# Audio tower on one Trainium2 core: first input in smaller pieces, weights issued by ScalarE, batch norm's output made by GpSimd

## Chip, cores and metric

The kernel runs on one core of a Trainium2 chip. The metric is the device time of one execution in microseconds (us); lower is better. Times of several executions are given as their median.

## What is computed

The reference passes x, 16 sequences of 750 steps with 64 features, through five layers. Only the first is touched here; for a sequence it is

```python
win = jnp.concatenate([x[:, i:i + 746, :] for i in range(5)], axis=-1)
y = jax.nn.relu(jnp.einsum('btk,ok->bto', win, W) + b)
mean = jnp.mean(y, axis=(0, 1))
var = jnp.mean(jnp.square(y - mean), axis=(0, 1))
h = (y - mean) * jax.lax.rsqrt(var + EPS) * gamma + beta
```

The window is five steps, so 746 steps of 128 features come out of each sequence. Mean and variance are over all sequences and steps, so no output can be made before the last sequence has been convolved. Then follow four residual layers, each on a layer norm of h: a delta-rule attention, a mixture of experts in which experts choose tokens, a cross-attention to video, and a second mixture of experts with two experts per token.

## The kernel before, in words

Everything stays in one core's on-chip memory. The phases run one after another, and each phase is one or more blocks; in a block each engine has its own program, and all engines, SyncE included, meet at its end. The change is in `conv_phase`, which has two blocks; `norm_phase` (line 269), and with it the rest of the kernel, follows.

**First block: the convolution.** The features lie on the partitions. x is loaded twice, one step apart, on partitions 0 to 63 and 64 to 127 (lines 103 and 104), so that one matmul handles two of the five steps. `xw` is the place of x, laid over the tensor `h` that the second block fills. SyncE issues first the eight `first_loads` (line 99: two weight tiles of 128 partitions, a third in two halves of 64, then bias, gamma and beta with one number on each of 128 partitions, and the identity of 128x128, in this order), then x in four pieces of four sequences, two loads a piece, then some 40 `rest_loads` for later phases (line 106), and at last the `zeroed_loads` (line 109), which wait for two memsets of GpSimd. The small loads count up the semaphore `w_in`, each piece of x its own semaphore `x_in`, which reaches 32 when both loads have landed.

The matmuls run in a reduced-precision form, and weights and x are therefore split into a high and a low part; three products are summed. ScalarE makes the high part of each sequence (`high`, line 155), VectorE the low part by a subtraction (`low`, line 178), both in rings of three. At the start VectorE waits for all eight small loads, splits the weights (lines 184 and 187), and makes low parts only after that. TensorE waits for the split and for each low part. ScalarE applies bias and Relu out of the accumulation banks (line 167), VectorE takes statistics of each half sequence (line 196). At the end the statistics are aggregated (line 199), ScalarE takes the square root (line 170), and VectorE makes the scale and the shift in four short operations (lines 201 to 208).

**Second block: normalise and turn.** For each of the 16 sequences `yn = yT * scale + shift` is made (line 232, VectorE, two buffers), TensorE turns it by six transposes (line 249) into one of two halves of the banks, ScalarE copies it into `h` in two instructions (lines 262 and 264), and VectorE takes six statistics for the coming layer norm (line 226). VectorE's program puts the statistics of sequence b - 2 behind `yn` of sequence b. The semaphores: `tr_ps` tells that a sequence is turned, `yn_ready` that `yn` is there, `h_stored` that it is copied; `tr_ps` and `h_stored` begin at 2. GpSimd does one thing: it clears the unused rows of the last chunk of `h` (line 219), for which ScalarE waits (`pads`) before its first copy. SyncE waits there until all rest loads have landed.

Of the kernel before, what the change touches and what calls it, by code (L numbers as in the profile page):

```python
# [7 lines left out]
ALU = mybir.AluOpType  # L8
ACT = mybir.ActivationFunctionType
# [5 lines left out]
B = 16  # L15
T_IN = 750
CTX = 5
T = T_IN - CTX + 1
C = 128
NC = 6  # L20
# [17 lines left out]
EPS = 1e-5  # L38
# [33 lines left out]
def conv_phase(nc, k):  # L72

    stack, sb, sem = phase_scope(nc, k)
    with stack:
        yT = sb("yT", [P, B, T])
        yn = sb("yn", [P, 2, TP])
# [6 lines left out]
        bmv = sb("bmv", [P, 2])  # L84
        bsc = sb("bsc", [P, 4])
        xw = k.h[:].rearrange("p b c d -> p (b c d)")[:, 0:B * T_IN].rearrange("p (b t) -> p b t", t=T_IN)
        x_in = [sem(f"x_in{q}") for q in range(4)]
        w_in, rest_in = k.w_in, k.rest_in
        conv_ps, conv_relu, stats = sem("conv_ps"), sem("conv_relu"), sem("conv_stats")
        bn_chain, bn_sqrt = sem("bn_chain"), sem("bn_sqrt")  # L90
        yn_ready, tr_ps, h_stored, pads = sem("yn_ready"), sem("tr_ps"), sem("h_stored"), sem("pads")
        counted, zeroed = sem("c_counted"), sem("b2_zeroed")
        qb = B // 4

        with nc.Block() as block:
            @block.sync
            def _(sp):
                for ap, dram in k.first_loads:
                    sp.dma_start(ap, dram).then_inc(w_in, 16)
                for q in range(4):  # L100
                    s = slice(q * qb, (q + 1) * qb)

                    sp.dma_start(xw[0:64, s, :], k.xT[:, s, :]).then_inc(x_in[q], 16)
                    sp.dma_start(xw[64:128, s, 0:T_IN - 1], k.xT[:, s, 1:T_IN]).then_inc(x_in[q], 16)
                for ap, dram in k.rest_loads:
                    sp.dma_start(ap, dram).then_inc(rest_in, 16)
                sp.wait_ge(zeroed, 2)
                for ap, dram in k.zeroed_loads:
                    sp.dma_start(ap, dram).then_inc(rest_in, 16)
# [38 lines left out]
            @block.scalar  # L148
            def _(act):
                def high(b):  # L150
                    if b % qb == 0:
                        act.wait_ge(x_in[b // qb], 32)
                    if b >= RING:
                        act.wait_ge(conv_ps, 2 * (b - RING) + 2)
                    nc.scalar.activation(xh[:, b % RING, :], xw[:, b, :], ACT.Copy).then_inc(x_high, 1)

                act.wait_ge(edged, 1)
                for b in range(2):
                    high(b)
                act.wait_ge(w_in, 16 * len(k.first_loads))  # L160
                for b in range(B):
                    if b + 2 < B:
                        high(b + 2)
                    for half in range(2):
                        act.wait_ge(conv_ps, 2 * b + half + 1)
                        at, wide = EVEN[half]
                        nc.scalar.activation(yT[:, b, at:at + wide], k.ps[:, b % 2 * 2 + half, 0:wide], ACT.Relu,
                                             bias=k.conv_b[:, 0:1]).then_inc(conv_relu, 1)
                act.wait_ge(bn_chain, 1)
                nc.scalar.activation(bsc[:, 0:1], bmv[:, 1:2], ACT.Sqrt, bias=k.eps[:, 0:1]).then_inc(bn_sqrt, 1)  # L170

            @block.vector
            def _(dve):
                def low(b):
                    dve.wait_ge(x_high, b + 1)
                    if b >= RING:
                        dve.wait_ge(conv_ps, 2 * (b - RING) + 2)
                    nc.vector.tensor_tensor(xl[:, b % RING, :], xw[:, b, :], xh[:, b % RING, :].bitcast(F32),
                                            ALU.subtract).then_inc(x_low, 1)

                nc.vector.memset(k.eps[:], EPS)
                dve.wait_ge(w_in, 16 * len(k.first_loads))
                for j, w in enumerate((k.wc01, k.wc23, k.wc4)):
                    nc.vector.tensor_copy(wc[:, j, 0, :], w[:, :]).then_inc(w_split, 1)
                dve.wait_ge(w_split, 3)
                for j, w in enumerate((k.wc01, k.wc23, k.wc4)):
                    nc.vector.tensor_tensor(wc[:, j, 1, :], w[:, :], wc[:, j, 0, :].bitcast(F32),
                                            ALU.subtract).then_inc(w_split, 1)
                for b in range(2):
                    low(b)  # L190
                for b in range(B):
                    if b + 2 < B:
                        low(b + 2)
                    for half in range(2):
                        dve.wait_ge(conv_relu, 2 * b + half + 1)
                        nc.vector.bn_stats(bst[:, 2 * b + half, :],
                                           yT[:, b, half * HALF_T:(half + 1) * HALF_T]).then_inc(stats, 1)
                dve.wait_ge(stats, 2 * B)
                nc.vector.bn_aggr(bmv[:, :], bst[:].rearrange("p a s -> p (a s)")).then_inc(bn_chain, 1)
                dve.wait_ge(bn_sqrt, 1)  # L200
                nc.vector.reciprocal(bsc[:, 1:2], bsc[:, 0:1]).then_inc(bn_chain, 1)
                dve.wait_ge(bn_chain, 2)
                nc.vector.tensor_tensor(bsc[:, 2:3], bsc[:, 1:2], k.gamma[:, 0:1], ALU.mult).then_inc(bn_chain, 1)
                dve.wait_ge(bn_chain, 3)

                nc.vector.tensor_tensor(bsc[:, 0:1], bmv[:, 0:1], bsc[:, 2:3], ALU.mult).then_inc(bn_chain, 1)
                dve.wait_ge(bn_chain, 4)
                nc.vector.tensor_tensor(bsc[:, 3:4], k.beta[:, 0:1], bsc[:, 0:1], ALU.subtract).then_inc(bn_chain, 1)
                dve.wait_ge(bn_chain, 5)

        with nc.Block() as block:
            @block.sync
            def _(sp):
                sp.wait_ge(rest_in, 16 * (len(k.rest_loads) + len(k.zeroed_loads)))

            @block.gpsimd
            def _(pool):

                nc.gpsimd.memset(k.h[96:128, :, NC - 1, :], 0.0).then_inc(pads, 1)

            @block.vector
            def _(dve):
                def stats(b):
                    dve.wait_ge(h_stored, b + 3)
                    for c in range(NC):
                        last = nc.vector.bn_stats(k.st[:, b * NC + c, :], k.h[:, b, c, :])
                    last.then_inc(counted, 1)


                for b in range(B):  # L230
                    dve.wait_ge(tr_ps, b + 1)
                    nc.vector.tensor_scalar(yn[:, b % 2, 0:T], yT[:, b, :], bsc[:, 2:3], bsc[:, 3:4],
                                            ALU.mult, ALU.add).then_inc(yn_ready, 1)
                    if b >= 2:
                        stats(b - 2)
                for b in range(B - 2, B):
                    stats(b)
                dve.wait_ge(counted, B)

            @block.tensor  # L240
            def _(pe):
                pe.sem_inc(tr_ps, 2)
                with pe.Fori(0, PAIRS) as i:
                    for par in range(2):
                        pe.wait_ge(yn_ready, i * 2 + (par + 1))
                        pe.wait_ge(h_stored, i * 2 + (par + 1))
                        for c in range(NC):
                            n = rows(c)
                            last = nc.tensor.transpose(k.psf[0:n, par * 1024 + c * P:par * 1024 + (c + 1) * P],
                                                       yn[:, par, c * P:c * P + n], k.ident[:, :])  # L250
                        last.then_inc(tr_ps, 1)

            @block.scalar
            def _(act):
                act.sem_inc(h_stored, 2)
                act.wait_ge(pads, 1)
                with act.Fori(0, PAIRS) as i:
                    for par in range(2):
                        b = i * 2 + par
                        act.wait_ge(tr_ps, i * 2 + (par + 3))  # L260
                        o = par * 1024
                        nc.scalar.activation(k.h[:, b, 0:NC - 1, :],
                                             k.psf[:, o:o + 5 * P].rearrange("p (c d) -> p c d", d=P), ACT.Copy)
                        nc.scalar.activation(k.h[0:LAST, b, NC - 1, :],
                                             k.psf[0:LAST, o + 5 * P:o + 6 * P], ACT.Copy).then_inc(h_stored, 1)
# [2140 lines left out]
```

## Time and profile before

| | us |
|---|---|
| median of 3 executions | 2277.52 |
| lowest, highest | 2276.15, 2278.78 |
| the profiled execution: its own time | 2272.64 |
| its span | 2270.8 |

```profile
span 2270.8 us, 54560 instructions
...
PE 2000.0 (88%) x20890; PEld 1776.8 (78%) x20890; DVE 1607.0 (71%) x4095; ACT 1070.6 (47%) x2698; POOL 604.2 (27%) x650
```

PE is TensorE's matmuls, PEld its weight loads, DVE VectorE, ACT ScalarE, POOL GpSimd, SP SyncE; a "q" behind a name is the engine's sequencer. All times in the trace are counted from the start of the span. Neighbouring instructions of one kind are merged in a timeline; "x6" behind them is their number, and the duration is that of all of them together. What stands in brackets is how long the engine sat idle before, and who released it. These shares are over the whole span; the two blocks in question take the first 105 us of it, so the busy shares of the whole say little about them.

### The profile page before, as it was taken

The page shows a single profiled execution, that of the slowest core. Times are in us where ns is not written, and L with a number is a line of the kernel's source. Part 1 is how long each engine was busy: PE and PEld are TensorE (multiplying, and loading weights), DVE is VectorE, ACT ScalarE, POOL GpSimd, SP SyncE. Part 2 cuts the span into 40 slices and gives each one's busy share as a digit, 9 for nine tenths or more (in the row PEclk, how much of TensorE's full clock was granted, in tenths as well). Part 3 has the DMA queues.
Part 4 walks back from the last instruction along what each step waited for, and adds up shares of the span by engine and source line. Part 5 has one row for each costly group of instructions (what it writes and reads, how often), then busy time and mean ns, then how long its engine had stood idle before and what let it go on. Part 6 is the DMA issues. An engine that isn't in the chain of part 4 may idle for free. (4 is left out here: it accounts for less than half of the span.)

```text
span 2270.8 us, 54560 instructions
## 1 busy us (share of the span) xinstructions
PE 2000.0 (88%) x20890; PEld 1776.8 (78%) x20890; DVE 1607.0 (71%) x4095; ACT 1070.6 (47%) x2698; POOL 604.2 (27%) x650
## 2 busy tenths in 40 slices
PE   6589999989646988886999999976999999999998
PEld 5488777778534877885777777766999999999998
DVE  4755555654583855565999999986777777777774
ACT  4433333332344555552677766743444444444443
POOL 0002222220015555520343333343212222221220
PEclk9899999999877999997999999997999999999999
DMA  8100000000211111100000000000000000000000
GB/s 185 44 1 12 11 12 11 12 10 1 73 56 38 44 34 39 41 18 1 3 3 3 3 3 3 3 2 1 8 14 7 7 7 14 7 7 14 7 8 15
DMA packets 80355, 44.50 MB, mean 20 GB/s; under 512 B 45801, under 2 KB 74025, under 8 KB 79753
## 3 DMA queue, kind: packets, MB, share of 16 engines
q1 hardware_dynamic: 74248, 29.53, 5.7%
q0 software_dynamic: 5888, 12.07, 2.0%
q8 instruction: 136, 2.23, 0.4%
q14 instruction: 83, 0.67, 0.1%
HBM read 27.20 MB, written 14.38 MB: 18 GB/s over the span
## 5 line engine op out<-in xcount | busy, mean ns | idle before, releaser
L2127 ACT ACTIVATE w<-banks,b 128x384 f32<-128x384 f32 (+1 forms) x512 | 259.6, 572 | 392.9 <-PE banks L2201 392.9
L2183 PE MATMUL banks<-w,w 128*128 128x128 f32 (+1 forms) x3072 | 364.1, 275 | 0.0
L2183 PEld LDWEIGHTS banks<-w,w 128*128 128x128 f32 (+1 forms) x3072 | 350.4, 189 | 9.1 <-issue 8.7
L1710 PE MATMUL banks<-qT,w 64*64 64x128 f32 (+1 forms) x4608 | 267.9, 269 | 13.2 <-DVE eb L1612 8.7
L1710 PEld LDWEIGHTS banks<-qT,w 64*64 64x64 f32 x4608 | 247.3, 134 | 31.0 <-issue 20.8
L1718 PE MATMUL banks<-eb,w 64*64 64x128 f32 (+1 forms) x4608 | 268.9, 270 | 1.0 <-DVE eb L1612 1.0
L1681 POOL TENSOR_TENSOR t<-eb 128x768 f32<-128x768 f32 x96 | 171.8, 1789 | 289.0 <-ACT eb L1658 286.4
L1718 PEld LDWEIGHTS banks<-eb,w 64*64 64x64 f32 x4608 | 244.1, 133 | 1.7 <-DVE eb L1612 1.5
L2024 DVE SCALAR_TENSOR_TENSOR h<-banks,t_wt,h 128x128 f32 (+3 forms) x672 | 183.6, 342 | 83.2 <-PE banks L2183 79.7
L1237 POOL DMA_INDIRECT xg<-xs,rowu x184 | 178.4, 970 | 131.7 <-DMA xg<-xs,rowu 87.8
L1612 DVE TENSOR_TENSOR eb<-eb,rd 128x1536 f32<-128x1536 f32 x96 | 210.9, 2196 | 2.3 <-ACT rd L1669 2.3
L2199 PE MATMUL banks<-t_xh,t_w1h 128*128 128x384 f32 (+1 forms) x512 | 182.5, 356 | 0.2 <-ACT w L2106 0.2
L2201 PE MATMUL banks<-t_xh,t_w1l 128*128 128x384 f32 (+1 forms) x512 | 171.5, 335 | 0.0
L2200 PE MATMUL banks<-t_xlo,t_w1h 128*128 128x384 f32 (+1 forms) x512 | 171.0, 334 | 0.0
L1607 DVE TENSOR_REDUCE nm<-banks 128x128 bf16<-128x1536 f32 x96 | 162.8, 1696 | 11.3 <-PE banks L1710 11.3
L2067 POOL TENSOR_TENSOR t_rstd<-t_nv,t_minus_half 128x6 f32<-128x6 f32 x48 | 63.7, 1326 | 399.6 <-DVE t_nv L1925 398.2
L1658 ACT ACTIVATE eb<-banks 128x512 f32<-128x512 f32 (+1 forms) x288 | 147.1, 586 | 0.5
L1183 DVE SCALAR_TENSOR_TENSOR x_yl<-banks,gates,x_yh 128x128 fp32r<-128x128 f32 x184 | 51.9, 344 | 134.1 <-ACT x_yh L1330 134.1
L1428 PE MATMUL banks<-x_sel,x_yh 128*128 128x374 f32 (+1 forms) x384 | 120.1, 395 | 2.1 <-DVE x_sel L1191 1.1
L1191 DVE TENSOR_SCALAR x_sel<-iota,place 128x748 fp32r<-128x748 f32 x184 | 105.2, 625 | 5.1 <-PE banks L1428 5.0
L729 ACT ACTIVATE DT<-banks 128x768 f32<-128x768 f32 x60 | 48.7, 811 | 123.4 <-PE banks L822 123.4
L1428 PE MATMUL banks<-x_sel,x_yl 128*128 128x374 f32 (+1 forms) x384 | 99.3, 340 | 0.0
(305 smaller groups left out, 4241.9 us busy)
## 6 DMA issues: line engine op xcount, KB each, us to landing
out<-h SPq DMA_DIRECT2D x16, 320.0 KB
xs<-r_xl SPq DMA_DIRECT2D x16, 192.0 KB, 2.6
h<-in_xT SPq DMA_DIRECT2D x4, 750.0 KB, 15.7
h<-in_xT SPq DMA_DIRECT2D x4, 749.0 KB, 18.6
xg<-xs,rowu POOLq DMA_INDIRECT x184, 2.5
xs<-r_xl SPq DMA_DIRECT2D x16, 128.0 KB
blocks<-NT SPq DMA_DIRECT2D x24, 48.0 KB, 1.9
D<-blocks SPq DMA_DIRECT2D x24, 48.0 KB, 2.0
```

The source lines that it names most:

```text
L1237: nc.gpsimd.indirect_dma_start(out=xg[:, 4 * g + j, :], out_offset=None, in_=k.xs, in_offset=bass.IndirectOffsetOnAxis(ap=rowu[:, col:col ...
L1428: last = nc.tensor.matmul(k.ps[:, 5 + s, 0:TW // 2], y[lo:hi, col % 8, :], sel[lo:hi, col % SEL, s * (TW // 2):(s + 1) * (TW // 2)], start ...
L1612: nc.vector.tensor_tensor(eb[:, w % 4, :, 0:m], eb[:, w % 4, :, 0:m], rd[:, w % 2, None, 0:m].to_broadcast([P, FR, m]), ALU.mult).then_inc ...
L1681: nc.gpsimd.tensor_tensor(t1[:, n % 2, 0:m, :].rearrange("p t v -> p v t"), e[:, 0:6, 0:m], e[:, 6:12, 0:m], ALU.add).then_inc(tree, 1)
L1710: last = nc.tensor.matmul(lbanks(n)[place(n, hd), v, 0:wide(n)], k.Kt[half(hd), v, :], qT[half(hd), n // NC % 2, (n % NC) * P:(n % NC) * P ...
L1718: last = nc.tensor.matmul(k.ps[half(hd), 6, 0:wide(a)], k.Vd[place(a, hd), v, half(hd)], eb[place(a, hd), a % 4, v, 0:wide(a)], start=(v = ...
L2024: last = nc.vector.scalar_tensor_tensor(out=hh, in0=k.psf[0:n, o:o + P], scalar=wt[0:n, par, c * E1 + e:c * E1 + e + 1], in1=hh if e else ...
L2127: nc.scalar.activation(gb[u % 2][:, f, s * GW:s * GW + NFREE[s]], k.ps[:, order.bank(n), 0:NFREE[s]], ACT.Relu, bias=k.b1_1[:, 2 * e + f:2 ...
L2183: last = nc.tensor.matmul(k.psf[0:n, o:o + P], gb[u % 2][:, f, c * P:c * P + n], k.w2_1[:, 2 * e + f, :], start=(f == 0), stop=(f == 1))
L2199: nc.tensor.matmul(ps, w1h[:, 2 * e + f, :], xh[:, g, 0:w], start=True, stop=False)
L2200: nc.tensor.matmul(ps, w1h[:, 2 * e + f, :], xlo[:, g, 0:w], start=False, stop=False)
L2201: nc.tensor.matmul(ps, w1l[:, 2 * e + f, :], xh[:, g, 0:w], start=False, stop=True).then_inc(full, 1)
```

## The change

In the first block SyncE issues x at once, in pieces of 1, 1, 2, 4, 4 and 4 sequences (12 loads). ScalarE issues the eight small loads as the first thing in its program, then waits for `eps` and takes a square root of it into a place that is overwritten later, and goes on as before. In the second block GpSimd makes `yn` for all 16 sequences. VectorE clears the unused rows of `h` and then only takes statistics.

```diff
--- before.py
+++ after.py
@@ -84,21 +84,20 @@
         bmv = sb("bmv", [P, 2])
         bsc = sb("bsc", [P, 4])
         xw = k.h[:].rearrange("p b c d -> p (b c d)")[:, 0:B * T_IN].rearrange("p (b t) -> p b t", t=T_IN)
-        x_in = [sem(f"x_in{q}") for q in range(4)]
+        x_in = [sem(f"x_in{q}") for q in range(6)]
         w_in, rest_in = k.w_in, k.rest_in
         conv_ps, conv_relu, stats = sem("conv_ps"), sem("conv_relu"), sem("conv_stats")
         bn_chain, bn_sqrt = sem("bn_chain"), sem("bn_sqrt")
         yn_ready, tr_ps, h_stored, pads = sem("yn_ready"), sem("tr_ps"), sem("h_stored"), sem("pads")
         counted, zeroed = sem("c_counted"), sem("b2_zeroed")
-        qb = B // 4
+        CUTS = (0, 1, 2, 4, 8, 12, B)
+        eps_set = sem("c_eps")
 
         with nc.Block() as block:
             @block.sync
             def _(sp):
-                for ap, dram in k.first_loads:
-                    sp.dma_start(ap, dram).then_inc(w_in, 16)
-                for q in range(4):
-                    s = slice(q * qb, (q + 1) * qb)
+                for q in range(len(CUTS) - 1):
+                    s = slice(CUTS[q], CUTS[q + 1])
 
                     sp.dma_start(xw[0:64, s, :], k.xT[:, s, :]).then_inc(x_in[q], 16)
                     sp.dma_start(xw[64:128, s, 0:T_IN - 1], k.xT[:, s, 1:T_IN]).then_inc(x_in[q], 16)
@@ -148,12 +147,16 @@
             @block.scalar
             def _(act):
                 def high(b):
-                    if b % qb == 0:
-                        act.wait_ge(x_in[b // qb], 32)
+                    if b in CUTS:
+                        act.wait_ge(x_in[CUTS.index(b)], 32)
                     if b >= RING:
                         act.wait_ge(conv_ps, 2 * (b - RING) + 2)
                     nc.scalar.activation(xh[:, b % RING, :], xw[:, b, :], ACT.Copy).then_inc(x_high, 1)
 
+                for ap, dram in k.first_loads:
+                    act.dma_start(ap, dram).then_inc(w_in, 16)
+                act.wait_ge(eps_set, 1)
+                nc.scalar.activation(bsc[:, 0:1], k.eps[:, 0:1], ACT.Sqrt)
                 act.wait_ge(edged, 1)
                 for b in range(2):
                     high(b)
@@ -178,7 +181,7 @@
                     nc.vector.tensor_tensor(xl[:, b % RING, :], xw[:, b, :], xh[:, b % RING, :].bitcast(F32),
                                             ALU.subtract).then_inc(x_low, 1)
 
-                nc.vector.memset(k.eps[:], EPS)
+                nc.vector.memset(k.eps[:], EPS).then_inc(eps_set, 1)
                 dve.wait_ge(w_in, 16 * len(k.first_loads))
                 for j, w in enumerate((k.wc01, k.wc23, k.wc4)):
                     nc.vector.tensor_copy(wc[:, j, 0, :], w[:, :]).then_inc(w_split, 1)
@@ -216,7 +219,10 @@
             @block.gpsimd
             def _(pool):
 
-                nc.gpsimd.memset(k.h[96:128, :, NC - 1, :], 0.0).then_inc(pads, 1)
+                for b in range(B):
+                    pool.wait_ge(tr_ps, b + 1)
+                    nc.gpsimd.tensor_scalar(yn[:, b % 2, 0:T], yT[:, b, :], bsc[:, 2:3], bsc[:, 3:4],
+                                            ALU.mult, ALU.add).then_inc(yn_ready, 1)
 
             @block.vector
             def _(dve):
@@ -227,13 +233,8 @@
                     last.then_inc(counted, 1)
 
 
+                nc.vector.memset(k.h[96:128, :, NC - 1, :], 0.0).then_inc(pads, 1)
                 for b in range(B):
-                    dve.wait_ge(tr_ps, b + 1)
-                    nc.vector.tensor_scalar(yn[:, b % 2, 0:T], yT[:, b, :], bsc[:, 2:3], bsc[:, 3:4],
-                                            ALU.mult, ALU.add).then_inc(yn_ready, 1)
-                    if b >= 2:
-                        stats(b - 2)
-                for b in range(B - 2, B):
                     stats(b)
                 dve.wait_ge(counted, B)
```

## Rows read from the trace of the kernel before

**Rows 1.** Busy time by stretches of 10 us; columns as in the first line

```profile
core 0: us, PE busy (x) PEld busy (x) DVE busy (x) ACT busy (x) POOL busy (x), PEclk, DMA share, GB/s
...
10.00:20.00 10.00, 1.27 (x4) 1.30 (x5) 2.36 (x3) 3.55 (x4) 0.00 (x0) 1.00 1.03 214
20.00:30.00 10.00, 10.00 (x50) 8.44 (x50) 4.02 (x7) 3.52 (x6) 0.00 (x0) 1.00 1.08 225
...
80.00:90.00 10.00, 5.25 (x36) 3.76 (x36) 10.00 (x42) 5.35 (x13) 0.00 (x0) 1.00 0.00 0
```

**Rows 2.** Timeline, 0 to 32 us: start, duration, engine, line, work; SPq issues loads

```profile
0.72 2.15 SPq L99 DMA_DIRECT2D wc<-in_L_tok_WT  x4
...
4.50 0.43 SPq L99 DMA_DIRECT2D ident<-in_ident  x1
4.97 0.47 SPq L103 DMA_DIRECT2D h<-in_xT  x1
...
6.51 1.35 DVE L184 CAST c_w<-wc 128x128 fp32r<-128x128 f32 x3 [5.66 <-DMA ident<-in_ident]
...
7.90 0.70 DVE L187 TENSOR_TENSOR c_w<-wc,c_w 128x128 fp32r<-128x128 f32 x3
...
15.48 1.28 ACT L155 ACT_TABLE_LOAD   x1 [15.48 <-DMA h<-in_xT]
...
16.78 2.27 ACT L155 ACTIVATE c_xh<-h 128x750 fp32r<-128x750 f32 x3
17.64 2.64 DVE L178 TENSOR_TENSOR c_xl<-h,c_xh 128x750 fp32r<-128x750 f32 x3 [9.05 <-ACT c_xh L155]
...
18.73 0.65 PE L132 MATMUL banks<-c_xh,c_w 128*128 128x374 f32 x1 [18.73 <-DVE c_xl L178]
```

**Rows 3.** Timeline, end of the convolution; last line: SyncE's waits, us in total, times, longest

```profile
65.64 0.36 SPq L109 DMA_DIRECT2D gate<-in_L_ffn_gate_weight  x1
...
69.78 1.28 ACT L170 ACT_TABLE_LOAD   x1
70.38 1.02 DVE L199 BATCH_NORM_AGGREGATE bmv<-bst 128x2 f32<-128x192 f32 x1
71.44 0.29 ACT L170 ACTIVATE bsc<-bmv,eps 128x1 f32<-128x1 f32 x1 [0.37 <-DVE bmv L199]
...
SPq L95 <- PEq L95: 6.8, 1, 6.8
```

**Rows 4.** Timeline, the second block

```profile
73.01 1.80 POOL L219 MEMSET h<- 32x2048 f32 x1 [65.30 <-POOLq L95]
...
78.17 1.26 DVE L226 BATCH_NORM_STATS2 st<-h 128x6 f32<-128x128 f32 x6 [0.64 <-ACT h L264]
...
79.91 1.25 DVE L226 BATCH_NORM_STATS2 st<-h 128x6 f32<-128x128 f32 x6
79.93 0.70 ACT L262 ACTIVATE h<-banks 128x640 f32 x1 [0.82 <-PE banks L249]
...
81.07 0.70 ACT L262 ACTIVATE h<-banks 128x640 f32 x1 [0.26 <-PE banks L249]
...
100.74 3.57 DVE L226 BATCH_NORM_STATS2 st<-h 128x6 f32<-128x128 f32 x18
```

**Rows 5.** Line 232 by itself: duration ns min/median/max, first and last start us

```profile
L232 DVE TENSOR_SCALAR yn<-yT,bsc x16: 648/652/2034, 73.2 to 100.2; 128x746 f32<-128x746 f32 x16
```

**Rows 6.** DMA from 8 to 16 us

```profile
DMA packets 368, 1.73 MB, mean 216 GB/s; under 512 B 32, under 2 KB 32, under 8 KB 288
```

**Rows 7.** The small loads of line 99, all eight

```profile
DMA to landing us min/median/max: 1.8/2.0/2.2
```

**Rows 8.** GpSimd's instructions by line and shape: count, busy us, mean ns, idle before

```profile
L1681 POOL TENSOR_TENSOR t<-eb 128x768 f32<-128x768 f32 x80 | 146.8, 1835 | 251.6 <-ACT eb L1658 249.0 <-DVE den L1603 2.6
L2067 POOL TENSOR_TENSOR t_rstd<-t_nv,t_minus_half 128x6 f32<-128x6 f32 x48 | 63.7, 1326 | 399.6 <-DVE t_nv L1925 398.2
...
L1469 POOL COPY vD<-vT 128x768 f32<-128x768 f32 x1 | 0.8, 823 | 58.9 <-ACTq L1464 58.9
```

## The prediction

> **What bounds the kernel now.** The change touches only the first two blocks of one phase, so the first view is the busy time by stretches of 10 us [rows 1]. Three things are to be seen. From 10 to 20 us TensorE does 1.27 us of work while the DMA engines are full: the start waits for data. From 20 to 30 us TensorE is busy all the time: the convolution is TensorE's. From 80 to 90 us VectorE is busy 10.00 of 10.00 us and TensorE about half: the second block is VectorE's. GpSimd is empty in all three.
>
> Second, the timeline of the start [rows 2]. SyncE issues eight small loads (weights, bias, gamma, beta, identity) from 0.72 to 4.93 us, and only then, from 4.97 us, eight loads of x, two for each piece of four sequences. The weights are there at 6.51 us, when VectorE starts to split them, and the split ends at 8.60 us. ScalarE waits for the first piece until 15.48 us, then loads an activation table for 1.28 us, and makes the first high part at 16.78 us; VectorE's first low part starts at 17.64 us and TensorE at 18.73 us. So x is last, with weights ready 9 us before.
>
> Third, the end of the convolution [rows 3]. ScalarE's table load for the square root (69.78 to 71.06 us) lies beside the last statistics and their aggregation, which ends at 71.40 us; the square root starts at 71.44 us. That load costs nothing today. SyncE had issued its last load at 66.0 us and waited 6.8 us for the others at the block's end: the first thing that could take over from a faster convolution.
>
> Fourth, the second block [rows 4, 5]. Each sequence costs VectorE a TENSOR_SCALAR and six statistics, and the pattern repeats every 1.74 us (78.17 to 79.91 us), 16 times; the last statistics end at 104.31 us.
>
> **Part 1: the start.** The x loads leave SyncE at 0.72 instead of 4.97 us, 12 issues now, and the first piece is one sequence (0.375 MB) instead of four (1.5 MB). The x stream ran at 1.73 MB in 8 us, 216 GB/s [rows 6], so 0.375 MB need 1.7 us alone, 3.5 us at half the rate. Small loads landed 2.0 us after issue [rows 7]; from 2.7 us on, the first sequence is in at 4.4 to 6.2 us. ScalarE has first to issue eight loads (4.2 us by SyncE's own row), load the table (1.28 us) and take one square root (0.29 us), which ends at about 6.5 us; its first high part (0.83 us) can end by about 7.5 us. The table load has moved from the path to a place where it is hidden behind the weights. If Copy or Relu needed another table, the 1.28 us would go into the same cover, or, before the first Relu, into the time that TensorE takes for the first sequence.
>
> So the **weights** become last: VectorE needs 2.1 us of splitting after them and 1.1 us from the first low part to TensorE [rows 2]. When they land the trace cannot say, because it has no such stretch. Lower end: 6.5 us as before, start at 9.7 us, 9.0 us won. Upper end: the eight loads have 896 partition rows (six of 128, two of 64), a packet each, 56 on each of 16 engines, and each waits for one packet of x; x packets took 8 us x 16 / 368 = 0.35 us [rows 6], so 56 x 0.35 = 19.5 us, landing near 22 us, start near 25.2 us, 6.5 us lost. I take a value near the lower end: by bytes the weights are 0.26 MB, at half the rate 2.4 us, less than the 4.2 us that their issue takes, so only the last one's wait counts: 8 packets per engine, each behind 3000 bytes of x (3000 bytes x 16 / 216 GB/s = 0.22 us), 1.8 us. With 2.0 us of latency the identity, issued at 4.5 us, lands at 8.3 us; I round to 8.5 us. TensorE then starts at 8.5 + 2.1 + 1.1 = 11.7 us: **7.0 us won**.
>
> [...]
>
> What follows doesn't shorten: the 16 sequences take 3.2 us each (18.7 to 70.4 us [rows 2, 3]), while x arrives every 1.75 us, so later pieces of 4 are early. The chain from last statistics to scale and shift keeps its length. SyncE's issues: x now streams from 2.7 instead of about 7 us but shares with the weights, so I expect its end to move by about 2.5 us, to 63.5 us; the block would end at 66.0 + 6.8 - 7.0 = 65.8 us. The cover is 2.3 us, and nearly gone if the weights land at 6.5 us: about 9 us is the most this part can give.
>
> **Part 2: the second block.** VectorE loses 16 TENSOR_SCALARs (0.65 us each [rows 5]) and takes one memset that GpSimd did in 1.80 us [rows 4]; ScalarE needs it only with its first copy 4 us into the block, so it is hidden. VectorE's 96 statistics remain: 18 in 3.57 us, 1.19 us per sequence. ScalarE's copies come every 1.14 us where they hardly wait (79.93 to 81.07 us). GpSimd now makes yn, with no row of its own for this operation. Lower end: its copy of 128x768, 0.82 us [rows 8]. Upper end: its two-input operation, 1.84 us for 768 elements [rows 8], so 1.79 us for 746. I take 1.0 us, nearest to the copy, because it too reads one tensor; with 0.1 us for the wait GpSimd's 1.1 us stays below VectorE's 1.2 us, so the exact value doesn't matter up to there. Its wait for transposes two sequences back holds nothing else, for its queue is otherwise empty.
>
> First sequence: today yn was ready at 75.2 us (its 2.03 us, beside GpSimd's memset, where the others take 0.65 [rows 5]), and the first statistics began 2.95 us later. Now GpSimd runs beside VectorE's memset; I allow it until 75.0 us. Statistics from 77.9 us, 16 x 1.2 = 19.2 us, end 97.1 us on the old clock, against 104.3: **7.2 us won**. With a first yn at 74.1 us it would be 8.1 us.
>
> **Sum:** 7.0 + 7.2 = 14.2 us. The profiled execution took 2272.64 us (2270.8 us of span and 1.8 us around it), 4.9 us below the median; the same difference taken from the median 2277.52 gives **2263.3 us**. Everything after waits at the blocks' ends, so I carry the sum through whole. The runs spread by 2.6 us; I count 0.2% (4.6 us) as what can be told from no change.
>
> **Rivals.**
> A, weights late: the packet-by-packet turn above. For it: 56 packets on each engine against a stream that fills them; against it: nothing but the small bytes. -6.5 + 7.2 = 0.7 us won, 2276.8 us. Chance 0.10.
>
> B, GpSimd becomes the bound: 1.79 us each. 73.2 + 16 x 1.89 = 103.4 us for the last yn, + 3.5 us for its transposes, copies and statistics (today from 100.8 to 104.3 us) = 106.9 us, 2.6 us later than today. 7.0 - 2.6 = 4.4 us won, 2273.1 us. For it: the only arithmetic on GpSimd near this size is the two-input row; against it: this operation reads half as much. At 1.4 us each 10.6 us would be won. Chance 0.17. [...]
>
> C, slower: GpSimd works through multiply and add as two passes, 2 x 1.79 = 3.58 us. 73.2 + 16 x 3.68 + 3.5 = 135.6 us, 31.3 us later; with 7.0 us won at the start 24.3 us slower, 2301.8 us. The time turns slower by 0.2% from 2.35 us each (73.2 + 16 x 2.45 + 3.5 = 115.9 = 104.3 + 7.0 + 4.6). For it: a power of only 6 elements takes GpSimd 1.33 us [rows 8], so an operation's kind can cost more than its size; against it: multiply and add are the simple kinds of its other rows. Chance 0.05.
>
> The change doing less than it says (another table load at the end or the start) is hidden, as shown.
>
> **Numbers.** Forecast 0.66; the remaining 0.02 is mishaps. Faster: the forecast, two thirds of B, and the part of A in which the weights land between the ends, 0.80; same 0.14; slower 0.06. Range: 9.0 + 8.1 us won and 2 us of spread give 2258; B and its spread give 2274; A's end and C stay outside.
>
> **To be seen afterwards.** TensorE's first matmul near 11.7 us and VectorE's first cast near 8.5 us right; a first cast past 15 us is A. The last statistics of the second block 24 us after its start; VectorE's statistics waiting for ScalarE's copy, and these for transposes waiting for GpSimd, is B or C, with GpSimd's mean as the price. If SyncE's last issue comes after the convolution's last statistics, the start's gain was capped there. An untouched part that changes its length by over 2 us would make the forecast wrong in a way I have not counted.

## The result: 5 us won where 14 were forecast

| | before | changed |
|---|---|---|
| median of 13 executions each | 2275.94 us | 2269.53 us |
| lowest, highest | 2269.11, 2278.97 | 2265.55, 2275.72 |
| the profiled execution, its span | 2270.8 | 2267.7 |
| first operation of the layer norm behind the two blocks | 105.23 us | 97.26 us |

The ratio on record is 0.9977, with a 95% interval of 0.9967 to 0.9988: 5.2 us (2.7 to 7.5) less, faster by just more than what I had set as telling (4.6 us). A ratio on record is not the quotient of the two medians, here 0.9972, and can differ from it by up to 0.001; gains of whole kernels are read from the ratios throughout. The time lies inside the forecast's range, but the change won less than half of the 14.2 us forecast, and by another balance. The two halves went opposite ways: the start lost, the second block won more than forecast.

The start of the changed kernel, from its timeline:

```profile
0.74 0.61 SPq L102 DMA_DIRECT2D h<-in_xT  x1
0.74 2.16 ACTq L157 DMA_DIRECT2D wc<-in_L_tok_WT  x4
...
4.67 0.67 ACTq L157 DMA_DIRECT2D ident<-in_ident  x1
...
5.37 1.28 ACT L159 ACT_TABLE_LOAD   x1 [5.37 <-issue]
...
6.77 0.81 ACT L154 ACTIVATE c_xh<-h 128x750 fp32r<-128x750 f32 x1
...
8.02 0.83 ACT L154 ACTIVATE c_xh<-h 128x750 fp32r<-128x750 f32 x1 [0.43 <-DMA h<-in_xT]
...
17.17 0.83 ACT L154 ACTIVATE c_xh<-h 128x750 fp32r<-128x750 f32 x1 [8.33 <-DMA ident<-in_ident]
17.17 1.35 DVE L187 CAST c_w<-wc 128x128 fp32r<-128x128 f32 x3 [16.30 <-DMA ident<-in_ident]
...
19.17 2.63 DVE L181 TENSOR_TENSOR c_xl<-h,c_xh 128x750 fp32r<-128x750 f32 x3
...
20.25 0.65 PE L131 MATMUL banks<-c_xh,c_w 128*128 128x374 f32 x1 [20.25 <-DVE c_xl L181]
```

The answer to [rows 2]. x is there early: ScalarE has its table by 6.65 us and the high parts of the first two sequences by 8.85 us. Then it sits for 8.33 us, and VectorE for 16.30 us, and the row names the load of the identity for both. VectorE splits from 17.17 us, against 6.51 us before, and TensorE starts at 20.25 us, 1.5 us *later* than before. The DMA view of the first 18 us shows why. A queue's row has its packets, its MB and the share of the 16 DMA engines' time that the packets took; the last number of a load is its time in us from issue to landing (of two loads the median):

```profile
q1 hardware_dynamic: 913, 3.32, 83.9%
q10 hardware_dynamic: 1024, 0.26, 8.5%
...
wc<-in_L_tok_WT ACTq DMA_DIRECT2D x2, 64.0 KB, 2.6
...
wc<-in_L_tok_WT ACTq DMA_DIRECT2D x2, 32.0 KB, 4.4
ident<-in_ident ACTq DMA_DIRECT2D x1, 64.0 KB, 12.5
...
conv_b<-in_L_tok_b ACTq DMA_DIRECT2D x1, 0.5 KB, 5.7
gamma<-in_L_tok_gamma ACTq DMA_DIRECT2D x1, 0.5 KB, 6.9
beta<-in_L_tok_beta ACTq DMA_DIRECT2D x1, 0.5 KB, 9.6
```

A second queue, q10, carries the small loads: 1024 packets, 0.26 MB. Its tiles land 2.6 and then 4.4 us after issue, bias 5.7, gamma 6.9, beta 9.6, the identity 12.5 us, where all eight took 1.8 to 2.2 us before [rows 7]. The same view from 10 to 14 us:

```profile
q1 hardware_dynamic: 117, 0.75, 87.4%
q10 hardware_dynamic: 122, 0.05, 7.7%
```

Queue against queue, 117 and 122 packets: one for one, though x's packets carry 0.75 MB and the small ones 0.05 MB. Elsewhere it was not one for one: from 2 to 6 us the view has 434 small packets to 307 of x, from 6 to 10 us 339 to 240, and from 14 to 17.2 us, with the last small ones, 52 to 217. From 2 to 17.2 us that is 947 to 881. The counts are over all 16 engines; no view shows one engine alone.

The end of the convolution and the second block, to be held against [rows 3 to 5]:

```profile
61.99 0.36 SPq L108 DMA_DIRECT2D gate<-in_L_ffn_gate_weight  x1
...
71.25 1.02 DVE L202 BATCH_NORM_AGGREGATE bmv<-bst 128x2 f32<-128x192 f32 x1
...
73.22 0.16 DVE L211 TENSOR_TENSOR bsc<-beta,bsc 128x1 f32<-128x1 f32 x1
74.13 1.94 POOL L224 TENSOR_SCALAR yn<-yT,bsc 128x746 f32<-128x746 f32 x2 [55.75 <-SPq L214]
74.37 1.76 DVE L236 MEMSET h<- 32x2048 f32 x1 [0.99 <-PEq L96]
...
77.75 18.99 DVE L232 BATCH_NORM_STATS2 st<-h 128x6 f32<-128x128 f32 x96 [1.61 <-ACT h L265]
...
97.26 0.33 DVE L298 TENSOR_TENSOR n0tmp<-st 128x96 f32<-128x96 f32 x1 [0.52 <-PEq L214]
```
```profile
L224 POOL TENSOR_SCALAR yn<-yT,bsc x16: 969/970/979, 74.1 to 90.5; 128x746 f32<-128x746 f32 x16
```

GpSimd makes all 16 yn in 0.97 us each. VectorE's 96 statistics, once they start, follow without a gap, 18.99 us, from 77.75 to 96.74 us. The block lasts 22.6 us from GpSimd's first operation, where it took 31.3. The layer norm starts 8.0 us earlier: 8.7 from the block and 0.4 from its end (the norm's first operation waits 0.52 instead of 0.92 us), less 0.9 us for the later convolution and 0.2 us at the passage between the blocks. The length of the second block repeats within 0.3 us in every run; the 0.9 us does not. With the start untouched, the run of the second block alone (below) had its scale and shift ready at 70.41 us, 2.1 us before the kernel before (72.51 us): such is the scatter of one execution's first block.

### The profile page after: what moved, and what is told of

Read it like the earlier page. It is cut to its first block and busy times, and to the rows that moved or that the text cites. A ratio compares the mean times of both kernels' runs of the same rounds, so it can differ in the third digit from the quotient of the medians.

```text
span 2267.7 us, 54558 instructions
## 1 busy us (share of the span) xinstructions
PE 2002.6 (88%) x20890; PEld 1778.6 (78%) x20890; DVE 1598.9 (71%) x4080; ACT 1068.2 (47%) x2698; POOL 617.8 (27%) x665
## 3 DMA queue, kind: packets, MB, share of 16 engines
q0 software_dynamic: 5888, 12.07, 2.0%
q10 hardware_dynamic: 1024, 0.26, 0.1%
```

## The experiments

Theory 1: the small loads wait because each DMA engine serves the two queues in turn, a packet of one for a packet of the other. Theory 2: x's load of the memory, whatever the packets, or being issued by ScalarE, holds them. Theory 3: part of the gain is lost in later phases. Ratios and single times are to be held against runs of the kernel before on the same chip, whose median was 2269.84 us beside the first four kernels, 2275.16 us (one run) beside the single pieces and the half packets, and 2270.13 us beside the last five.

### One half at a time

The second block alone: the kernel before with the second block of the changed one.

```diff
second block of the kernel before:
-                nc.gpsimd.memset(k.h[96:128, :, NC - 1, :], 0.0).then_inc(pads, 1)
+                for b in range(B):
+                    pool.wait_ge(tr_ps, b + 1)
+                    nc.gpsimd.tensor_scalar(yn[:, b % 2, 0:T], yT[:, b, :], bsc[:, 2:3], bsc[:, 3:4],
+                                            ALU.mult, ALU.add).then_inc(yn_ready, 1)
...
```

> The kernel before with the second block alone changed (GpSimd makes yn, VectorE the memset and the statistics). All theories of the start: first matmul at 18.7 us as before. The second block takes 23 us instead of 31.3 us, the layer norm's first operation comes 8.0 us earlier, and the kernel is 8.0 us faster than before, a ratio of 0.9965. Theory 3: the ratio stays nearer to 1 than 0.9975, though the layer norm begins 8 us earlier.

Measured: 2263.43 us, ratio 0.9967 (0.9952 to 0.9982), 7.5 us less. The start is the old one in its order (first matmul at 18.04 us, where the kernel before had 18.73 us), the block lasts 22.6 us, and the layer norm starts at 94.26 us. Of the 11.0 us that this is earlier, 9.1 us are the block and its end, the rest is the scatter of the first block.

The start alone: the first block of the changed kernel with the second block of before.

```diff
second block of the changed kernel:
-                for b in range(B):
-                    pool.wait_ge(tr_ps, b + 1)
-                    nc.gpsimd.tensor_scalar(yn[:, b % 2, 0:T], yT[:, b, :], bsc[:, 2:3], bsc[:, 3:4],
-                                            ALU.mult, ALU.add).then_inc(yn_ready, 1)
+                nc.gpsimd.memset(k.h[96:128, :, NC - 1, :], 0.0).then_inc(pads, 1)
...
```

> The changed start (pieces of 1, 1, 2, 4, 4, 4, small loads from ScalarE, early table) with the second block as before. Theory 1: the small loads land near 17 us again, TensorE starts at 20.3 us against 18.7 us, the block ends 0.9 us later, and the kernel is 0 to 1.5 us slower than before: the same within what can be told. If the late weights came from the second block's code in some way (they should not), they would land near 6.5 us here and the kernel would be 9 us faster.

Measured: 2270.87 us, ratio 1.0004 (0.9990 to 1.0018); split at 17.21 us, first matmul at 20.29 us, the layer norm at 106.43 us, 1.2 us later than before. No gain of the start as it was built can be seen, and the 7.5 us of the second block alone cover the whole gain.

### Where the small loads are kept

The small loads back on SyncE, ahead of x:

```diff
             def _(sp):
+                for ap, dram in k.first_loads:
+                    sp.dma_start(ap, dram).then_inc(w_in, 16)
                 for q in range(len(CUTS) - 1):
...
-                for ap, dram in k.first_loads:
-                    act.dma_start(ap, dram).then_inc(w_in, 16)
                 act.wait_ge(eps_set, 1)
```

> The changed kernel with one part undone: SyncE issues the eight small loads again, ahead of x; the pieces of 1, 1, 2, 4, 4, 4, the early table and GpSimd's yn stay. Theory 1 (two queues take turns on the DMA engines, and the small packets each wait for one of x): with one queue and the small loads first, they land at 6.5 us as in the kernel before, VectorE's split ends at 8.6 us, the first piece lands near 9 us, TensorE starts near 10.2 us instead of 20.25 us, and the kernel takes 9 to 10 us less than the changed one. Theory 2 (x's load of the memory, not the second queue, holds the weights back): they land well after 6.5 us here too. Theory 3 (what is won in the first 100 us is partly lost in later phases): TensorE starts near 10 us, but the total falls by clearly less than 9 us against the changed kernel.

```profile
6.52 1.35 DVE L187 CAST c_w<-wc 128x128 fp32r<-128x128 f32 x3 [5.65 <-DMA ident<-in_ident]
...
9.00 0.83 ACT L156 ACTIVATE c_xh<-h 128x750 fp32r<-128x750 f32 x1 [6.76 <-DMA h<-in_xT]
...
10.94 0.65 PE L133 MATMUL banks<-c_xh,c_w 128*128 128x374 f32 x1 [10.94 <-DVE c_xl L181]
```

Measured: 2256.53 us, ratio 0.9933 (0.9913 to 0.9953). The timeline rows show the weights at 6.52, x's first sequence at 9.00 and TensorE at 10.94 us. Against the changed kernel 9.3 us came off the first matmul but 8.0 us off the layer norm's start (89.26 us); the rest is the subject of the tail below. By the two ratios it is 10 us faster than the changed kernel, as expected.

The loads left exactly where the change put them, and only the wait divided:

```diff
...
-                pool.wait_ge(w_in, 16 * len(k.first_loads))
+                pool.wait_ge(w_in, 48)
...
+                for n, (ap, dram) in enumerate(k.first_loads):
+                    act.dma_start(ap, dram).then_inc(wt_in if n < 4 else b_in if n == 4 else w_in, 16)
-                for ap, dram in k.first_loads:
-                    act.dma_start(ap, dram).then_inc(w_in, 16)
...
-                act.wait_ge(w_in, 16 * len(k.first_loads))
+                act.wait_ge(b_in, 16)
...
-                dve.wait_ge(w_in, 16 * len(k.first_loads))
+                dve.wait_ge(wt_in, 64)
...
+                dve.wait_ge(w_in, 48)
                 dve.wait_ge(bn_chain, 2)
```

> The changed kernel, loads issued exactly as there (same engines, order, packets), but the wait divided: VectorE splits the weights when the four weight tiles have landed, ScalarE's first Relu waits for the bias alone, VectorE's scale for gamma and beta, GpSimd's cast for the identity. In the changed kernel's trace the last of the four tiles lands 4.4 us after its issue, near 6.7 us, the bias near 8.6 us, the identity at 17.2 us. Theory 1 says that each load waits for as many turns as it has packets in front of it: split from about 6.9 us, TensorE at 10 to 10.5 us, 9 to 10 us less than the changed kernel. If instead all small loads are held together until x's first pieces are in, the tiles land after 13 us too, and little is won.

```profile
7.08 0.50 DVE L187 CAST c_w<-wc 128x128 fp32r<-128x128 f32 x3 [6.21 <-DMA wc<-in_L_tok_WT]
...
9.30 0.65 PE L131 MATMUL banks<-c_xh,c_w 128*128 128x374 f32 x1 [9.30 <-DVE c_xl L181]
...
17.11 0.29 POOL L115 CAST identb<-ident 128x128 bf16<-128x128 f32 x1 [16.25 <-DMA ident<-in_ident]
```

Measured: 2254.28 us, ratio 0.9933 (0.9911 to 0.9952). The last row is GpSimd's cast of the identity, released at 17.11 us as in the changed kernel; but the tiles were there for VectorE at 7.08 us, and TensorE starts at 9.30 us, 11 us earlier. So the tiles were in early though the queue ended late, and it was the wait for all eight that made everyone late.

x in 16 pieces of one sequence, so that its longest packet has 3000 instead of 12000 bytes (from 0 to 18 us the changed kernel's view has 86 packets of 8 KB and more, this run's none):

```diff
-        CUTS = (0, 1, 2, 4, 8, 12, B)
+        CUTS = tuple(range(B + 1))
```

> The changed kernel with x in 16 pieces of one sequence, so that no packet of x is longer than 3000 bytes; in the changed kernel the lower half's packets of a piece of four have 12000 bytes. The small loads are unchanged. If they wait by turns, a packet for a packet, whatever its length, shorter packets of x mean shorter turns: from 10 us on, where 174 small packets took 7.2 us, they need about a third, and the identity lands near 13 us instead of 17.2 us. If they wait for bytes or for x's first pieces as a whole, it lands at 17 us again. SyncE's issue of 32 loads of 0.6 us ends near 20 us; x then still comes faster than TensorE takes it.

```profile
q10 hardware_dynamic: 1024, 0.26, 8.2%
...
ident<-in_ident ACTq DMA_DIRECT2D x1, 64.0 KB, 6.0
```

The same 1024 small packets, but the identity now takes 6.0 us instead of 12.5, and VectorE splits from 10.71 us. One execution took 2262.26 us, the layer norm started at 90.48 us. That is further than expected (13 us), in the same direction: x's packets took 0.18 us of an engine each from 6 to 10 us here (329 packets in 92.2% of 16 engines' 4 us), against 0.26 us (240 in 97.3%) and then, from 10 to 14 us, 0.48 us (117 in 87.4%) in the changed kernel. The memory was loaded no less, 209 GB/s over the first 18 us against 199 in the changed kernel.

The tiles and the identity in twice the rows, for the same bytes: 1408 instead of 896 rows, 88 instead of 56 if they are spread evenly over the 16 DMA engines. The three waits count 13 loads:

```diff
-                    act.dma_start(ap, dram).then_inc(w_in, 16)
+                    w = ap.shape[-1]
+                    if w == C:
+                        act.dma_start(ap[:, 0:64], dram[:, 0:64]).then_inc(w_in, 16)
+                        act.dma_start(ap[:, 64:C], dram[:, 64:C]).then_inc(w_in, 16)
+                    else:
+                        act.dma_start(ap, dram).then_inc(w_in, 16)
```

> The changed kernel with the four weight tiles and the identity each loaded in two halves of 64 columns: the same bytes, but 256-byte packets, 88 instead of 56 on each DMA engine, and 13 loads instead of 8. If small packets wait by turns, the last one lands in proportion to the packets, after 20 us or more, and TensorE starts as much later. If the bytes set it, it lands near 17 us, or later only by the 2.5 us that five more issues take on ScalarE.

```profile
29.71 1.35 DVE L192 CAST c_w<-wc 128x128 fp32r<-128x128 f32 x3 [28.84 <-DMA ident<-in_ident]
...
32.79 0.65 PE L131 MATMUL banks<-c_xh,c_w 128*128 128x374 f32 x1 [32.79 <-DVE c_xl L186]
```

Its DMA view from 14 to 18 us:

```profile
q1 hardware_dynamic: 249, 0.95, 111.3%
q10 hardware_dynamic: 248, 0.00, 6.0%
```

The last small load lands at 29.7 instead of 17.2 us and TensorE starts 12.5 us later, with not one byte more, and from 14 to 18 us the queues again go one for one, 249 to 248. With 1616 instead of 1024 small packets for the same 0.26 MB, it was the packets that counted here, not the bytes. (The last issue comes at 8.0 instead of 4.7 us; that is a part of it, and it also moves more of the small packets beside x's long ones. From its own issue the last load took 21.7 instead of 12.5 us.) One execution took 2277.29 us.

Last, ScalarE keeps issuing the small loads, and x is kept from them:

```diff
                     s = slice(CUTS[q], CUTS[q + 1])
+                    if q == 2:
+                        sp.wait_ge(w_in, 16 * len(k.first_loads))
```

> The changed kernel with one wait added: SyncE issues the first two pieces of x (one sequence each), then waits for all eight small loads, and only then issues the rest. ScalarE issues the small loads as in the changed kernel, on its own queue, all waits for them undivided. Theory 1: what keeps the small loads is x's packets in the other queue, and two pieces have only 16 on each DMA engine; after these the small loads are alone and the last lands 2 to 3 us after its issue at 4.7 us, near 7 us, so that TensorE starts near 10.2 us. Rival: being issued by ScalarE, or on a second queue, is slow in itself; then the identity lands well after 8 us though nothing competes with it. The third piece is issued near 7 us and should land near 11 us, before TensorE has finished two sequences.

```profile
4.54 0.45 ACTq L159 DMA_DIRECT2D ident<-in_ident  x1
...
7.84 0.47 SPq L104 DMA_DIRECT2D h<-in_xT  x1
7.85 1.35 DVE L189 CAST c_w<-wc 128x128 fp32r<-128x128 f32 x3 [6.98 <-DMA ident<-in_ident]
...
10.93 0.65 PE L133 MATMUL banks<-c_xh,c_w 128*128 128x374 f32 x1 [10.93 <-DVE c_xl L183]
```

The identity, issued at 4.54 us by ScalarE, is in by 7.85 us, and TensorE starts at 10.93 us. The third piece of x reached ScalarE at 13.66 us, later than expected, and TensorE was still at the first two sequences. The eight small loads, on q10 again, landed 1.8 to 4.7 us after issue, the identity 3.3 us, with x's two single pieces beside them (up to 12.5 us in the changed kernel): neither ScalarE nor the second queue was slow by itself. The other half of theory 2, the load of the memory, fell with the single pieces: 209 against 199 GB/s, and the identity in after 6.0 instead of 12.5 us. One execution took 2251.16 us.

### The two other edits of the start

Both were made on the kernel with the small loads on SyncE. Pieces of four again:

```diff
-        CUTS = (0, 1, 2, 4, 8, 12, B)
+        CUTS = (0, 4, 8, 12, B)
```

> The kernel with the small loads on SyncE ahead of x, with x in four pieces of four sequences again; the early table and GpSimd's yn stay. It is the kernel before with the table moved and the second block changed. Theory 1: the size of the first piece is what the start gains from: x's first piece is in at 15.5 us, without a table load behind it TensorE starts at 17.4 us, 6.5 us after its start with single pieces (10.94 us), and 1.3 us before that of the kernel before.

```profile
14.85 2.27 ACT L156 ACTIVATE c_xh<-h 128x750 fp32r<-128x750 f32 x3 [12.62 <-DMA h<-in_xT]
...
16.80 0.65 PE L133 MATMUL banks<-c_xh,c_w 128*128 128x374 f32 x1 [16.80 <-DVE c_xl L181]
```

No early table:

```diff
-                act.wait_ge(eps_set, 1)
-                nc.scalar.activation(bsc[:, 0:1], k.eps[:, 0:1], ACT.Sqrt)
```

> The kernel with the small loads on SyncE ahead of x, without the early square root, so that ScalarE loads a table when x's first piece has landed (9.0 us) and another before the square root. Once the weights are early the first load is on the path again: TensorE starts at 12.2 us instead of 10.94 us. The second is hidden behind the aggregation as before. In the changed kernel, whose weights land at 17.17 us, the early table is worth nothing.

```profile
8.82 1.28 ACT L156 ACT_TABLE_LOAD   x1 [8.82 <-DMA h<-in_xT]
...
12.07 0.65 PE L133 MATMUL banks<-c_xh,c_w 128*128 128x374 f32 x1 [12.07 <-DVE c_xl L179]
```

So the small first piece is worth 5.9 us of start (16.80 against 10.94 us) and the early table 1.1 us (12.07 against 10.94), as long as the weights don't come last. One execution of each took 2255.16 and 2256.56 us; single executions of this kernel differ by more than these effects, so only the timelines are read here.

### SyncE's tail

In the kernel with the small loads on SyncE, the first block's end looks like this, and so it does with divided waits:

```profile
63.19 0.16 DVE L211 TENSOR_TENSOR bsc<-beta,bsc 128x1 f32<-128x1 f32 x1
65.13 0.36 SPq L110 DMA_DIRECT2D gate<-in_L_ffn_gate_weight  x1
66.13 1.94 POOL L224 TENSOR_SCALAR yn<-yT,bsc 128x746 f32<-128x746 f32 x2 [58.40 <-PEq L243]
```
```profile
62.00 0.16 DVE L212 TENSOR_TENSOR bsc<-beta,bsc 128x1 f32<-128x1 f32 x1
62.28 0.36 SPq L108 DMA_DIRECT2D gate<-in_L_ffn_gate_weight  x1
63.28 1.94 POOL L225 TENSOR_SCALAR yn<-yT,bsc 128x746 f32<-128x746 f32 x2 [45.07 <-PEq L244]
```

Each fence's first row is VectorE's last operation on the scale, the second SyncE's last load, the third GpSimd's first yn. GpSimd starts 0.64 us after SyncE's last issue has ended in both, but 2.8 us after VectorE in one and 1.1 us in the other: SyncE now ends the block. Ten of its loads were moved to the second block, on both kernels:

```diff
-                for ap, dram in k.rest_loads:
+                for ap, dram in k.rest_loads[:-3]:
                     sp.dma_start(ap, dram).then_inc(rest_in, 16)
-                sp.wait_ge(zeroed, 2)
-                for ap, dram in k.zeroed_loads:
-                    sp.dma_start(ap, dram).then_inc(rest_in, 16)
...
+                sp.wait_ge(zeroed, 2)
+                for ap, dram in k.rest_loads[-3:] + k.zeroed_loads:
+                    sp.dma_start(ap, dram).then_inc(rest_in, 16)
                 sp.wait_ge(rest_in, 16 * (len(k.rest_loads) + len(k.zeroed_loads)))
```

> The kernel with the small loads on SyncE ahead of x, and the same ten loads moved into the second block. There VectorE's last scale operation ended at 63.35 us and SyncE's last issue at 65.49 us, GpSimd's first yn came at 66.13 us. If SyncE's issue held the block's end, GpSimd now starts near 64.1 us and the kernel takes 2.0 us less than without the move. If the block's end has another cause, the start stays at 66.1 us.

```profile
64.02 0.16 DVE L208 TENSOR_TENSOR bsc<-beta,bsc 128x1 f32<-128x1 f32 x1
64.69 0.33 SPq L216 DMA_DIRECT2D w<-in_L_ffn_w1T  x1
64.94 1.94 POOL L224 TENSOR_SCALAR yn<-yT,bsc 128x746 f32<-128x746 f32 x2 [57.26 <-PEq L243]
```

And the same move in the kernel with divided waits:

> The kernel with divided waits, and SyncE's last ten loads (three of the rest loads, two of them of 1 MB, and the seven that wait for the memsets) moved from the first block into the second. With divided waits alone VectorE's last scale operation ended at 62.16 us while SyncE's last issue ended at 62.64 us, and GpSimd's first yn came at 63.28 us. If SyncE's issue held the block's end, GpSimd starts 0.75 us after VectorE's last operation, as in the changed kernel, at 62.9 us: 0.4 us won, which a timing can't tell. The second block has room: ten issues take about 11 us of its 23 us. If the loads disturb the second block, it ends later than 23 us after its start.

With the small loads on SyncE the first yn comes at 64.94 instead of 66.13 us, 0.76 us after VectorE's last operation, and the layer norm at 88.07 instead of 89.26 us: 1.2 us won, not 2.0, because this execution's convolution ended 0.8 us later. Time 2255.15 us, ratio 0.9931 (0.9914 to 0.9948), against 0.9933: not to be told apart. With divided waits the first yn comes at 63.17 instead of 63.28 us and the layer norm at 86.30 instead of 86.20 us: the move shows no gain there. Its time is 2251.28 us, ratio **0.9913** (0.9897 to 0.9929), 19.7 us less than before: the lowest ratio of this study, clearly better than both kernels, but not to be told apart from divided waits alone.

### Is anything lost later?

The layer norm started earlier than in the kernel before by 8.0 us in the changed kernel, 11.0 with the second block alone, 16.0 with the small loads on SyncE, 19.0 with divided waits, 18.9 with the tail moved as well; the ratios stand for 5.2, 7.5, 15.2, 15.2 and 19.7 us. The last three agree within their intervals (some 4 us to either side). The first two lie just above theirs (7.5 and 10.9 us), but all five are counted from one execution of the kernel before, whose convolution, from first matmul to the shift, was the longest of all thirteen profiled: 53.8 us, where the others took 52.4 to 53.6 in no order. So theory 3 isn't needed, though a loss of 1 or 2 us in later phases isn't excluded.

In the changed kernel's own profile only 3.1 us of the 8.0 are left at the end. Mostly this is SyncE's wait in one later block, that of the experts' token gathers, which was 254.5 us long against 247.9 us. In the eleven other executions profiled here, whose code is the same from there on, this wait lies anywhere from 245.9 to 252.0 us. I take it for scatter of the execution, though nothing here shows its source. It is a reason to take a gain of 8 us from the stretch that changed and not from one total.

## Why the prediction was right and wrong

- **When the weights land** is the step that failed: "so only the last one's wait counts", 8.5 us. I let each small load clear while the next was being issued. They didn't clear: from bias to identity the time to landing grew with every load (5.7, 6.9, 9.6, 12.5 us), and x's packets took longer as its pieces grew from one sequence to four, 0.18 us of an engine each from 2 to 6 us (307 packets in 85.7% of 16 engines' 4 us), 0.26 from 6 to 10 and 0.48 from 10 to 14 us. Rival A came nearest, 56 small packets on an engine, each behind one of x, with a first cast past 15 us as its mark: the cast came at 17.17 us. Its size was too large: 17.2 us, not 22, for until 10 us more small packets went than x's, 1.4 for one (why, no run shows). The queue carried 1024 packets in the end, 128 more than the 896 rows; in the run with 13 loads it carried 1616, 208 more than the 1408. So there are 16 packets for each load beyond its rows; what they are for, no run shows. I gave the rival 0.10 because the bytes are few; but with the same 0.26 MB in 1616 instead of 1024 packets the last load took 21.7 instead of 12.5 us to land. Issuing from ScalarE took 4.2 us of issue off SyncE's queue ahead of x, and VectorE's split began 10.7 us later for it. The weights came at 17.17 instead of 8.5 us, and the start cost 1.5 us at the first matmul where 7.0 were to be won. With -1.5 in the place of 7.0 the forecast's own sum reads 5.7 us, and 7.2 us with the second block as it came out; 5.2 (2.7 to 7.5) were measured.
- **The early table and the small piece** did what was said. In the changed kernel both are hidden behind the late weights; where the weights are early they are worth 1.1 and 5.9 us of start.
- **What follows** was right: TensorE kept its pace of about 3.2 us a sequence, and the chain to scale and shift its length (2.2 us from the last statistics, before and changed).
- **SyncE's end** was forecast at 63.5 us; it came at 62.35 us. The cap was foreseen for early weights and showed as such: with divided waits 62.64 us against VectorE's 62.16, with the small loads on SyncE 65.49 against 63.35 us.
- **The second block** was right, and a little small: GpSimd took 0.97 us (1.0 forecast), VectorE 1.19 us per sequence, as forecast. The 8.7 us instead of 7.2 come mostly from the first sequence: I had let GpSimd's first yn be held up beside VectorE's memset until 2.0 us into the block, and it took 0.97 us like all others; another 0.25 us came off the way from there to the first statistics. Rivals B and C fell with that price.
- **The sum** was carried through whole, and as far as can be told rightly: the second block alone won 9.1 us up to the layer norm, and its ratio stands for 7.5 us (4.1 to 10.9). That the total fell inside the range was no merit of the working: 1.5 us of too small a second block and a range that reached down to rival B made room for a start that went the other way.

## What to carry to other kernels

A few small loads beside a stream of large ones waited by packets here, not by bytes (with the same 0.26 MB in 1616 instead of 1024 packets the last load took 21.7 instead of 12.5 us to land): count the rows of the small loads per DMA engine, multiply by what one packet of the stream takes (an upper end: 22 us by this count, 17.2 measured), and keep them ahead of the stream, or start on those that came first. A semaphore that counts all loads makes everyone as late as the last (17.17 us, where the tiles were there at 7.08 us); one for each group of users cost nothing that shows here and was worth 11 us of start. After a start has been shortened, look at what else must end with the block: here it was the queue of an engine that computes nothing (SyncE's last issue ended at 65.49 us, VectorE's last operation at 63.35 us).

## What was not expected of the hardware

Where GpSimd and VectorE got into each other's way, only VectorE was seen to be slowed. VectorE's first yn took 2.03 us beside GpSimd's memset of 1.80 us, and 0.65 us alone [rows 5]. VectorE's three casts of the weights took 1.35 us in all wherever GpSimd's cast of the identity and its memset ran at the same time, and 0.50 us in the two kernels with divided waits, where GpSimd still waited. GpSimd's cast of the identity took 0.29 us in both cases, and its yn, next to VectorE's memset and statistics, 968 to 983 ns in every run that has it. VectorE's statistics were not slowed beside yn, which ran for most of their time: 96 took 18.99 us, and 18 took 3.57 us with GpSimd idle [rows 4], 0.20 us each both times. So these rows show who was slowed, but not whether that is a matter of direction or of the kind of operation: no run has GpSimd's yn beside a cast or a yn of VectorE's.
